# One of eight groups of a block's probabilities turned by a DMA transpose of its f16 halves, the other seven by TensorE

## The reference, cut to what matters

```python
# layer 0: mask = adj > 0
agg   = mask @ x / max(row_sum(mask), 1)
x     = layernorm(x + relu(concat(x @ W_self + b_self, agg @ W_nb + b_nb) @ W_comb + b_comb))
# layer 1
neib_att = tanh(neigh @ Wn1 + bn1) @ Wn2 + bn2          # 4096 x 32, once
value    = neigh @ Wv + bv                              # 4096 x 128, once
x_att    = tanh(x @ Wx1 + bx1) @ Wx2 + bx2
ws       = leaky_relu(x_att @ neib_att.T, 0.01)
ws       = softmax(where(adj > 0, ws, -9e15), axis=1)   # 4096 x 4096
out      = layernorm(x + concat(x @ Wfx + bfx, ws @ value))
```

## Time and profile before

| what | before |
|---|---|
| median of 3 runs | 750.91 us (749.74 to 750.93) |
| the profiled execution's own time | 749.63 us |
| its span | 747.8 us |
| PE, PEld busy | 713.9 us (95%), 617.3 us (83%) |
| DVE busy | 622.2 us (83%) |
| ACT busy | 585.0 us (78%) |
| POOL busy | 111.7 us (15%) |
| mean DMA share | 73.5% on SP's queue |
| chain that ended last | PE 87%, DVE 4%, ACT 4%, issue 3%, DMA 1%, POOL 1% |

### The profile page before, as it was taken

One profiled execution on the slowest core, in us unless ns is written; L12 is line 12 of the kernel. 1 busy time (PEld: TensorE's weight loads), 2 busy tenths in 40 slices (PEclk: granted clock), 3 DMA queues, 4 the chain that ended last, 5 costly groups with the idle time before them and its releaser, 6 DMA issues.

```text
span 747.8 us, 20493 instructions
## 1 busy us (share of the span) xinstructions
PE 713.9 (95%) x7600; PEld 617.3 (83%) x7600; DVE 622.2 (83%) x1599; ACT 585.0 (78%) x1080; POOL 111.7 (15%) x241
## 2 busy tenths in 40 slices
PE   5989989999999999999999999999999999999785
PEld 4556668998899889889899889988988988988564
DVE  4887578888898888888888889888888888888874
ACT  2455248888888888888888888888888888889995
POOL 0010121111111111111111111111111111111201
PEclk9989999999999999999999999999999999999999
DMA  8976999988787867888988888787879888620000
GB/s 273 369 170 132 250 268 198 192 186 185 158 181 153 192 167 168 170 172 184 191 191 186 180 162 180 172 160 176 173 169 174 184 192 192 128 51 10 8 8 15
DMA packets 192564, 124.64 MB, mean 167 GB/s; under 512 B 157777, under 2 KB 176081, under 8 KB 192465
## 3 DMA queue, kind: packets, MB, share of 16 engines
q1 hardware_dynamic: 192020, 123.31, 73.5%
q10 hardware_dynamic: 444, 0.02, 0.0%
HBM read 81.35 MB, written 4.19 MB: 114 GB/s over the span
## 4 chain that ended last, share of the span: by engine, by line
PE 87%; DVE 4%; ACT 4%; issue 3%; DMA 1%; POOL 1%; SPq 0%; POOLq 0%; ACTq 0%; DVEq 0%
PE ps_v L1079 21%; PE ps_agg L1042 14%; PE ps_agg L1045 14%; PE ps_t L1066 14%; PE ps_s L1057 7%; PE ps_agg L1097 3%; PE ps_agg L1100 3%; PE ps_s L956 2%; PE ps_v L964 2%; PE ps_x L1117 1%; PE ps_x L1120 1%; PE ps_t L947 1%; PE ps_agg L1088 1%; ACT score L872 1%; PE ps_x L1111 1%
## 5 line engine op out<-in xcount | busy, mean ns | idle before, releaser
L1042 PE MATMUL ps_agg<-x,mask_t 128*128 128x257 f16 x1024 | 243.3, 273 | 0.2 <-DMA mask_t<-mask 0.2
L865 ACT ACTIVATE score<-ps_s,sc 128x512 f32<-128x512 f32 x256 | 177.0, 692 | 81.3 <-PE ps_s L1057 79.6
L1045 PE MATMUL ps_agg<-x,mask_t 128*128 128x256 f16 x1024 | 237.4, 273 | 0.3 <-DVE x L494 0.3
L1079 PEld LDWEIGHTS ps_v<-v,late 128*128 128x128 f16 x3072 | 191.1, 97 | 45.9 <-DVE late L717 15.4
L1079 PE MATMUL ps_v<-v,late 128*128 128x128 f16 x3072 | 213.5, 219 | 8.6 <-DVE late L717 7.0
L717 DVE TENSOR_TENSOR late<-ps_t,late 128x512 f16<-128x512 f32 x256 | 175.0, 684 | 55.8 <-ACT late L878 53.9
L653 DVE CUSTOM_DVE_ANT_0 score<-score,mask 128x512 f32<-128x512 f32 x256 | 175.8, 687 | 9.4 <-ACT score L865 9.0
L878 ACT CAST late<-ps_t 128x512 f16<-128x512 f32 x256 | 148.6, 580 | 15.0 <-PE ps_t L1066 15.0
L872 ACT ACTIVATE score<-score,exp_bias,sc 128x1024 f32<-128x1024 f32 x128 | 158.1, 1235 | 1.6 <-DVE exp_bias L662 1.6
L1066 PE MATMUL ps_t<-ident,score 128*128 128x128 f32 x1024 | 155.8, 275 | 3.7 <-ACT score L872 3.5
L1045 PEld LDWEIGHTS ps_agg<-x,mask_t 128*128 128x128 fp8e4 x1024 | 100.4, 98 | 16.0 <-issue 5.3
(11 more groups left out here) (130 smaller groups left out, 723.4 us busy)
## 6 DMA issues: line engine op xcount, KB each, us to landing
adj_sb<-in_adj_dram SPq DMA_DIRECT2D x128, 512.0 KB, 5.3
neigh_sb<-in_L_gnn_neigh_dram SPq DMA_DIRECT2D x8, 512.0 KB, 8.1
score<-in_x_dram SPq DMA_DIRECT2D x8, 512.0 KB, 8.5
x_in<-in_x_dram SPq DMA_DIRECT2D x32, 128.0 KB, 2.3
out_dram<-out_sb SPq DMA_DIRECT2D x32, 128.0 KB, 3.1
mask_t<-mask SPq DMA_TRANSPOSE x128, 4.7
mask<-in_L_gnn_W_comb_dram SPq DMA_DIRECT2D x1, 512.0 KB, 8.7
x_t<-x SPq DMA_TRANSPOSE x32, 4.4
```

The lines of the kernel that those rows point to most:

```text
L865: act.activation(score[:, b % 2, k * GW:(k + 1) * GW], ps_s[k % 2][:, :], ACT.Prelu, alpha=SLOPE, scale=score_scale).then_inc(leaky_made, 1)
L1042: mm = pe.matmul(agg[:, 0:D + 1], mask_t8[:, c, 0, :], x16[:, c, X_HI:X_ONE + 1], start=(c == 0), stop=(c == NC - 1), skip_group_check=True)
L1045: mm = pe.matmul(agg[:, 0:D], mask_t8[:, c, 0, :], x16[:, c, X_LO:X_LO + D], start=False, stop=False, skip_group_check=True)
L1079: mm = pe.matmul(ps_v[:, 0:DV], p[:, k % 2, chunk], v16[:, c, v:v + DV], start=(c == 0 and part == 0), stop=(c == NC - 1 and part == 2))
```

## The change

For one of the eight groups of each block, group 0, the turning moves from PE to a DMA.

- ACT (`wide_high`, slot 34) copies the group's probabilities from `score` in SBUF to f16, the high half; DVE (`wide_low`, slot 36) subtracts it from `score` and writes the low half beside it. SP (`turn_wide`, slot 37) issues one DMA transpose of the 128x1024 f16 of both halves into `wide_t`. The two tiles lie in the room of `neigh_sb` that is no longer used.
- PE turns groups 1 to 7 only, in slots 33 to 39, so that slot 40 of a block (class 0) has no turning. The seven come first in the weighing (slots 34 to 40), and the group from the DMA comes last (slot 41). PE still has 12 matmuls for it.
- `p_high` and `p_low` are there for seven groups. The exponentials are taken in slots 32, 33, 35 and 37 in place of 32, 34, 36 and 38, as group 1 now is the first to be turned and group 2 the second.
- Waits: ACT's `leaky` of group 0 waits for `wide_low` of two blocks ago; `wide_high` waits for the transpose of the block before to have landed; `turn_wide` waits for `wide_low` and for the weighing of the block before; PE's last weighing of a block waits for the transpose.

The core of the diff:

```diff
+BY_DMA = 1
+BY_PE = NG - BY_DMA
+EXPS_OF_WIDE = 1
+EXPS = ((0, 0), (1, 1), (3, 2), (5, 3))
+WIDE_HIGH_AT = 34
+WIDE_LOW_AT = 36
+WIDE_TURN_AT = 37
...
+def turned_by_pe(s, at):
+    d = due(s, at)
+    return (*d, d[0] * BY_PE + d[1]) if d and d[1] < BY_PE else None
...
+            def turn_wide(b):
+                sp.wait_ge(wide_lo_made, b + 1)
+                at_least(sp, pv_done, NG * b)
+                for h in range(BY_DMA):
+                    part = slice(h * CQ, (h + 1) * CQ)
+                    sp.dma_start_transpose(wide_t[:, :, :, :].rearrange("p a c n -> p (a c) n")[:, part, :],
+                                           wide[:, h * QW:(h + 1) * QW]).then_inc(wide_t_in, 16)
...
+            def wide_low(b):
+                dve.wait_ge(wide_hi_made, b + 1)
+                dve.tensor_tensor(wide_p[:, 1, :], score[:, b % 2, 0:BY_DMA * GW], wide_p[:, 0, :],
+                                  ALU.subtract).then_inc(wide_lo_made, 1)
...
+            def wide_high(b):
+                act.wait_ge(exp_made, NQ * b + EXPS_OF_WIDE)
+                at_least(act, wide_t_in, 16 * BY_DMA * b)
+                act.copy(wide_p[:, 0, :], score[:, b % 2, 0:BY_DMA * GW]).then_inc(wide_hi_made, 1)
...
-                if d := due(s, ROW_MAX_AT + 1):
-                    if d[1] % 2 == 0:
-                        exps(d[0], d[1] // 2)
-                if d := due(s, TURN_AT):
+                for at, q in EXPS:
+                    if d := due(s, ROW_MAX_AT + 1 + at, 0):
+                        exps(d[0], q)
+                if d := due(s, WIDE_HIGH_AT, 0):
+                    wide_high(d[0])
+                if d := turned_by_pe(s, TURN_AT):
                     p_high(*d)
...
-            def turn_p(b, k):
-                if k % 2 == 0:
-                    pe.wait_ge(exp_made, NQ * b + k // 2 + 1)
-                at_least(pe, p_lo_made, NG * b + k - 1)
+            def turn_p(b, j, n):
+                k = BY_DMA + j
+                pe.wait_ge(exp_made, NQ * b + [q for _, q in EXPS].index(k // 2) + 1)
+                at_least(pe, p_lo_made, n - 1)
...
-            def weigh_values(b, k):
-                pe.wait_ge(p_lo_made, NG * b + k + 1)
+            def weigh_values(b, j):
+                if j < BY_PE:
+                    pe.wait_ge(p_lo_made, BY_PE * b + j + 1)
+                elif j == BY_PE:
+                    pe.wait_ge(wide_t_in, 16 * BY_DMA * (b + 1))
...
+                    if j < BY_PE:
+                        c, n = (BY_DMA + j) * CG + u, BY_PE * b + j
+                        hi, lo = (p[:, n % 2, u * P:(u + 1) * P] for p in (p_hi, p_lo))
+                    else:
+                        c = (j - BY_PE) * CG + u
+                        hi, lo = wide_t[:, 0, c, :], wide_t[:, 1, c, :]
```

More of the change, by code:

```diff
@@ L172, in gnn_kernel @@
         mv2 = sb("mv2", [P, 5], F32)
+        wide = neigh_sb[:, 0:2 * BY_DMA * GW // D, :].rearrange("p b d -> p (b d)").bitcast(F16)
+        wide_p = wide[:, 0:2 * BY_DMA * GW].rearrange("p (a n) -> p a n", a=2)
+        wide_t = wide[:, 2 * BY_DMA * GW:4 * BY_DMA * GW].rearrange("p (a c n) -> p a c n", a=2, c=BY_DMA * CG)
         def turned(turn, dc):
@@ L280, in gnn_kernel @@
         p_hi_made = sem("p_hi_made")
+        wide_hi_made = sem("wide_hi_made")
+        wide_lo_made = sem("wide_lo_made")
+        wide_t_in = sem("wide_t_in")
         x1_hi_made = sem("x1_hi_made")
@@ L381, in _ @@
                     turn_x(d[0])
+                if d := due(s, WIDE_TURN_AT, 0):
+                    turn_wide(d[0])
                 if d := due(s, LAYER0_AT + 1, 0):
@@ L713, in add_fx, with p_low @@
                                          in1=res[:, b % RES_BUFS, 0:DV], op0=ALU.mult, op1=ALU.add).then_inc(res_made, 1)
-            def p_low(b, k):
-                dve.wait_ge(p_hi_made, NG * b + k + 1)
-                dve.tensor_tensor(p_lo[:, k % 2, :], ps_t[k % 2][:, :], p_hi[:, k % 2, :],
+            def p_low(b, j, n):
+                dve.wait_ge(p_hi_made, n + 1)
+                dve.tensor_tensor(p_lo[:, n % 2, :], ps_t[n % 2][:, :], p_hi[:, n % 2, :],
                                   ALU.subtract).then_inc(p_lo_made, 1)
+            def wide_low(b):
+                dve.wait_ge(wide_hi_made, b + 1)
+                dve.tensor_tensor(wide_p[:, 1, :], score[:, b % 2, 0:BY_DMA * GW], wide_p[:, 0, :],
+                                  ALU.subtract).then_inc(wide_lo_made, 1)
             def row_scale(b):
@@ L768, in _ @@
                         make_mask(d[0], q)
-                if d := due(s, TURN_AT):
+                if d := due(s, WIDE_LOW_AT, 0):
+                    wide_low(d[0])
+                if d := turned_by_pe(s, TURN_AT):
                     p_low(*d)
@@ L863, in leaky @@
                 act.wait_ge(s_done, NG * b + k + 1)
-                at_least(act, pt_done, NG * (b - 2) + k + 1)
+                if k < BY_DMA:
+                    at_least(act, wide_lo_made, b - 1)
+                else:
+                    at_least(act, pt_done, BY_PE * (b - 2) + k - BY_DMA + 1)
                 act.activation(score[:, b % 2, k * GW:(k + 1) * GW], ps_s[k % 2][:, :], ACT.Prelu, alpha=SLOPE,
@@ L873, in exps, with p_high @@
                                accum_out=sums[:, b % 2, q:q + 1]).then_inc(exp_made, 1)
[L875 to L878, removed]
+            def p_high(b, j, n):
+                act.wait_ge(pt_done, n + 1)
+                at_least(act, pv_done, NG * b + j - 1 if j >= 2 else NG * (b - 1) + BY_PE + j - 1)
+                act.copy(p_hi[:, n % 2, :], ps_t[n % 2][:, :]).then_inc(p_hi_made, 1)
+            def wide_high(b):
+                act.wait_ge(exp_made, NQ * b + EXPS_OF_WIDE)
+                at_least(act, wide_t_in, 16 * BY_DMA * b)
+                act.copy(wide_p[:, 0, :], score[:, b % 2, 0:BY_DMA * GW]).then_inc(wide_hi_made, 1)
             def normalise1(b):
@@ L1058, in scores @@
                           stop=True).then_inc(s_done, 1)
-            def turn_p(b, k):
-                if k % 2 == 0:
-                    pe.wait_ge(exp_made, NQ * b + k // 2 + 1)
-                at_least(pe, p_lo_made, NG * b + k - 1)
+            def turn_p(b, j, n):
+                k = BY_DMA + j
+                pe.wait_ge(exp_made, NQ * b + [q for _, q in EXPS].index(k // 2) + 1)
+                at_least(pe, p_lo_made, n - 1)
                 for u in range(CG):
                     at = k * GW + u * P
-                    mm = pe.transpose(ps_t[k % 2][:, u * P:(u + 1) * P], score[:, b % 2, at:at + P], ident[:, :])
+                    mm = pe.transpose(ps_t[n % 2][:, u * P:(u + 1) * P], score[:, b % 2, at:at + P], ident[:, :])
                 mm.then_inc(pt_done, 1)
-            def weigh_values(b, k):
-                pe.wait_ge(p_lo_made, NG * b + k + 1)
-                if k == 0:
+            def weigh_values(b, j):
[3 more added lines that the diff above has]
+                    pe.wait_ge(wide_t_in, 16 * BY_DMA * (b + 1))
+                if j == 0:
                     at_least(pe, l1_step, 6 * (b - 1) + 4)
@@ L1075, in weigh_values @@
                 for u in range(CG):
[L1076 to L1080, removed]
+                    if j < BY_PE:
+                        c, n = (BY_DMA + j) * CG + u, BY_PE * b + j
+                        hi, lo = (p[:, n % 2, u * P:(u + 1) * P] for p in (p_hi, p_lo))
+                    else:
+                        c = (j - BY_PE) * CG + u
+                        hi, lo = wide_t[:, 0, c, :], wide_t[:, 1, c, :]
+                    for part, (p, v) in enumerate(((hi, 0), (hi, DV), (lo, 0))):
+                        mm = pe.matmul(ps_v[:, 0:DV], p, v16[:, c, v:v + DV],
+                                       start=(j == 0 and u == 0 and part == 0),
+                                       stop=(j == NG - 1 and u == CG - 1 and part == 2))
                 mm.then_inc(pv_done, 1)
```

2 lines of the change are left out of this document (1 added, 1 removed).

## The result

The changed kernel takes 737.23 us in the median of 4 runs (736.88 to 737.32), against 750.6 before (749.74 to 750.93): a ratio of 0.9823, 95% interval 0.9806 to 0.984. The profiled execution took 737.13 us with a span of 735.3, so 12.5 less than the one before (749.63).

What follows compares the result with a forecast made beforehand. PE, busy without a gap at 20.27 us a block, was taken as the bound. 749.63 - 12.1, all other terms 0, gave 737.5 us profiled; forecast 738.0, own range 735.5 to 740, wider range to 742.5.

Steps and rivals of the forecast that it cites:

- What PE saves: In class 0, one turning per block leaves PE, costing it 0.45 us: 27 x 0.45 = 12.1 us saved.
- the rival of 720 us: The transposes' whole duration is saved on PE: 27 x 4 x 0.275 = 29.7 us; chance 1 in 100.
- What ACT pays: New SBUF cast 0.8 us, 0.2 more a block; second exponentials 0.4 us to spare before class 2; sum 0.
- Rival 1: At class 2, late ACT makes PE wait up to 0.45 us a block: 738 to 750; 12 in 100.
- What DVE pays: In class 4, a subtraction with two SBUF inputs replaces one from PSUM, fitting in 1.41 us idle; sum 0.
- What SP and the DMA pay: Behind class 4's store: transpose issue 1.23 us, median landing 4.7 us, load 1.44 us, cover 5.7 us; time 0.
- Rival 2: PE waits for the transpose in class 1, or mask transposes if DMA bounds: 774 or 806; 5 in 100.
- Start and tail: First block: perhaps one PE wait; tail: 0.8 us more ACT, one chain fewer; taken 0, ends -1.5 and +2.

## Why the prediction was right

- *What PE saves* was the term that made the forecast, and it was right in mechanism and size: 27 x 0.45 = 12.1 expected, 11.9 measured, 11.2 taken back by four transposes a block. The duration of a transpose (275 ns, the rival of 720 us) would have given two and a half times as much.
- *What ACT pays*: the new cast takes 0.65 us (0.8 taken, ends 0.60 and 1.23). The spare time ahead of class 2 is 0.3 us (0.4 expected; the prediction left out the read of the sums). That the change hangs on the earlier exponentials is shown by the kernel with the old slots, though class 2, which the prediction took for the tightest place, has only 1.7 of its 5.8 us of waits. Rival 1 did not occur.
- *What DVE pays*: 0.69 us in the idle time of class 4, as said.
- *What SP and the DMA pay*: issue behind the store, the load of x not pushed enough to matter, the mask's transpose not at all. The load per block, 0.89 x 19.83 - 0.79 x 20.27 = 1.6 us, is the lone 1.44 us within the rounding of the shares; with three more it is 1.45 us each. The landing is 3.6 us in the median where 4.7 was taken. Rival 2 was built on a share that cannot exceed the block, and that step was wrong: with three more transposes the share is 1.12 at the same time. Its other leg, a late landing, is real, with the edge between slots 37 and 39.
- *Start and tail* was taken as 0, and here the sum was off. The start lost 0.3 us (the one wait that was forecast) and 0.9 by scatter. The tail gained 1.8, beyond the end of -1.5, and not by the reason given: in the last block PE still waits 0.73 us for the halves ahead of its last group from PSUM. It gained earlier, and not from PE's time, as two kernels show. Where exactly stays open.
- The sum was 737.5 for the profiled execution, 737.13 was measured; for the median 738.0 and 737.23. That it lies so near is in part luck: the 1.2 us lost at the start and the 1.8 gained in the tail nearly cancel, and neither was in the sum. The 1.3 us that the runs before lay above their profiled one did not show here (736.88 to 737.32, the profiled one 737.13).

## What to carry to other kernels

Where one engine is busy without a gap, price an instruction by the distance from its start to the next start, and look for work to move off that engine; then follow the engine that feeds it slot by slot, since a table that moves its steps by one slot can cost many times the gain. A DMA busy share near 1 is not by itself a bound: ask where the hollows lie and whose landing has how many slots of cover. A mechanism must be tested by itself even where its number comes out: the two groups by DMA took the time of the wrong rival.

## What the runs showed of the hardware that was not expected

POOL's busy time rose from 111.7 to 130.2 us with the same 241 instructions. One of its steps of 128x1 elements took 0.27 us before and takes 0.77 now (mean of 27), which is 13.6 us:

```profile
398.00 0.77 POOL L471 TENSOR_SCALAR mv<-mv 128x1 f32<-128x1 f32 x1
```

At that moment DVE begins a subtraction with two inputs in SBUF:

```profile
398.03 0.69 DVE L686 CUSTOM_DVE_ANT_0 score<-score,mask 128x512 f32<-128x512 f32 x1
```

In the kernel before this step of POOL (L438, 402.55 to 402.82) met the same kind of instruction, which began at 402.69, only in its last 0.14 us. By the Trainium skill ("SBUF — State Buffer", Who interferes with whom) such a pair contends; the prediction looked for it on DVE, where 0.69 us is what it always took, and it is POOL that pays. The kernel before shows it already: the same step, an addition to 128x1 elements, takes 0.62 us in the second norm, beside a DVE instruction with both inputs in SBUF, and 0.22 in the first, beside one with an input in PSUM.

```profile
401.02 0.69 DVE L653 CUSTOM_DVE_ANT_0 score<-score,mask 128x512 f32<-128x512 f32 x1
401.18 0.62 POOL L434 TENSOR_SCALAR mv<-mv 128x1 f32<-128x1 f32 x1 [6.68 <-DVE mv L741]
...
410.83 0.66 DVE L717 TENSOR_TENSOR late<-ps_t,late 128x512 f16<-128x512 f32 x1
411.00 0.22 POOL L420 TENSOR_SCALAR mv<-mv 128x1 f32<-128x1 f32 x1 [8.19 <-DVE mv L691]
```

Most of what is left of the rise is POOL's sum of two 128x256 tiles (L429 before, L462 now). In the kernel before, the changed one and the first with two groups it starts some 0.5, 0.35 and 0.1 us after such an instruction of DVE and takes 0.74, 0.92 and 1.17 us, so that it ends 0.6 us after DVE's in all three. It costs nothing here, since POOL has idle time behind it. That POOL waits until DVE's instruction is over is read from these rows, and from how the durations move from kernel to kernel with the start; no kernel was made to try it by itself.

PE's granted clock fell from 1.00 to 0.90 on average in a kernel where PE pauses for 2.25 to 5.03 us once a block, and to 0.95 to 0.97 in one where it pauses for 1.6 to 2.5 us three times a block. There a pause of 1.58 or 1.69 us left it at 1.00, and one of 2.51 us was followed by 0.50 or 0.51 in 11 of 16 blocks.
